# Value products of local attention one tile later and amid the step, scores at its end; the feed-forward mean, variance and broadcast in the other bank

## What is computed

```
def attn_layer(x, Wqkv, qs, ksc, Wo):
    q, k, v = split(x @ Wqkv)                 # 16 heads of 64
    q = l2norm(q) * qs;  k = l2norm(k) * ksc
    q, k = rotary(q), rotary(k)
    out = local_attention(q, k, v)            # windows of 32: 32 queries see 64 keys
    return out @ Wo
def ffn_layer(x, g, bln, W1, b1, W2, b2):
    xn = (x - mean(x)) / sqrt(var(x) + 1e-05) * g + bln
    a, gate = split(xn @ W1 + b1)             # 2 x 341
    return a * gelu(gate) @ W2 + b2
for i in range(6):
    x = attn_layer(shift_tokens(x), ...) + x
    x = ffn_layer(shift_tokens(x), ...) + x
```

## Time and profile before

| | |
|---|---|
| median of three runs | 3652.7 us (3648.79 to 3658.39) |
| profiled execution | 3656.53 us, its span 3654.8 us |
| PE busy | 3287.4 us, 90% of the span |
| DVE / POOL / ACT busy | 2817.2 / 2340.6 / 2230.3 us (77 / 64 / 61%) |
| granted TensorE clock | 0.961 of full speed on average |
| stretches | first stack about 40 to 1700 us, global attention to about 1970 us, second stack about 1975 to 3645 us |

### The profile page before, as it was taken

The page is one execution under the profiler, slowest core; times in us unless marked ns, Lnnn a source line. Parts: engine busy times, 40 slices in busy tenths (PEclk is TensorE's granted clock), DMA queues, the critical chain, the costliest instruction groups (busy, mean ns, idle before and its releaser), DMA issues. The chain is left out here.

```text
span 3654.8 us, 147212 instructions
## 1 busy us (share of the span) xinstructions
PE 3287.4 (90%) x61692; PEld 2149.2 (59%) x61692; DVE 2817.2 (77%) x4178; ACT 2230.3 (61%) x3970; POOL 2340.6 (64%) x2167
## 2 busy tenths in 40 slices
PE   5899999999999999996897899989999999999996
PEld 2566666666666666663223566666666666666664
DVE  4788888887887888882344788877877788888883
ACT  3566676765665666662774566665666566666663
POOL 4677787776776777772003677666666667777761
PEclk8999999999999999997998899999999999999997
DMA  3234334334334333320001233323323333333321
GB/s 118 74 92 112 87 92 117 86 85 115 80 87 112 82 91 97 84 72 18 21 1 31 69 77 93 81 72 92 79 74 92 76 77 94 86 78 96 82 73 32
DMA packets 216859, 289.96 MB, mean 79 GB/s; under 512 B 61068, under 2 KB 105864, under 8 KB 215304
## 3 DMA queue, kind: packets, MB, share of 16 engines
q1 hardware_dynamic: 216200, 280.54, 29.8%
HBM read 43.43 MB, written 10.49 MB: 15 GB/s over the span
## 5 line engine op out<-in xcount | busy, mean ns | idle before, releaser
L1166 POOL TENSOR_TENSOR rot<-t 128x512 f32<-128x512 f32 x768 | 975.1, 1273 | 309.4 <-DVE t L1025 289.7
L1172 POOL TENSOR_TENSOR qkn<-rot,rn 128x512 f32<-128x512 f32 x768 | 793.1, 1043 | 174.7 <-DVE rn L1048 174.7
L1024 DVE TENSOR_TENSOR t<-duo,table 128x512 f32<-128x512 f32 x768 | 526.5, 686 | 156.0 <-ACT sq L854 144.4
L1178 POOL TENSOR_TENSOR prob<-prob,rsum 128x512 f32<-128x512 f32 x192 | 297.0, 1547 | 417.7 <-DVE rsum L1067 417.0
L1025 DVE TENSOR_TENSOR t<-duo,table 128x512 f32<-128x512 f32 x768 | 522.4, 680 | 0.0
L693 PE MATMUL sv_all<-pT,arena 64*64 64x32 f32 x24576 | 419.7, 221 | 82.8 <-issue 82.7
L625 PE MATMUL duo<-w_pair,in_hi 128*128 128x512 f16 x1152 | 452.1, 392 | 34.6 <-POOL in_lo L1193 15.7
L860 ACT ACTIVATE arena<-duo 128x512 f32<-128x512 f32 x384 | 226.8, 591 | 403.5 <-PE duo L627 400.5
L854 ACT ACTIVATE sq<-duo 128x512 f32<-128x512 f32 x768 | 443.7, 600 | 39.9 <-PE duo L627 38.5
L649 PE MATMUL duo<-ident,qkn 128*128 128x128 f32 x3072 | 456.6, 280 | 9.0 <-issue 6.9
L1031 DVE TENSOR_REDUCE n<-sq 128x16 f32<-128x1024 f32 x384 | 464.3, 1209 | 0.0
(11 more groups left out here) (125 smaller groups left out, 5002.8 us busy)
## 6 DMA issues: line engine op xcount, KB each, us to landing
arena<-arena SPq DMA_DIRECT2D x1152, 128.0 KB, 2.4
arena<-arena SPq DMA_DIRECT2D x768, 64.0 KB, 2.0
w_pair<-w_split SPq DMA_DIRECT2D x44, 256.0 KB, 4.2
w_stage<-in_L_ffn_Wqkv SPq DMA_DIRECT2D x6, 1536.0 KB, 8.6
w_split<-split SPq DMA_DIRECT2D x30, 256.0 KB, 2.6
wo_sb<-in_L_ffn_Wo SPq DMA_DIRECT2D x12, 512.0 KB, 4.2
xsh<-xs SPq DMA_DIRECT2D x48, 128.0 KB, 2.5
f_in<-xs SPq DMA_DIRECT2D x48, 128.0 KB, 2.2
```

The source lines that it names most:

```text
L1024: dve.tensor_tensor(t1[:, b, :].rearrange("p (h d) -> p h d", d=DH), src, cos, ALU.mult)
L1166: pool.tensor_tensor(rot[:, c, :], t1[:, c % 2, :], t2[:, c % 2, :], ALU.add).then_inc(pool_add, 1)
L1172: pool.tensor_tensor(qkn[:, 0, c, :].rearrange("p (h d) -> p h d", d=DH), rot[:, c, :].rearrange("p (h d) -> p h d", d=DH), rn[:, c, :].un ...
```

## The change

It moves work between steps and inside a step; the arithmetic is the same.

- `turn_prob` and `outputs` take tile T - 3 instead of T - 2. `turn_prob` comes right after projection 0, `outputs` after `turn_qk` 1 and ahead of projection 2. `scores` stays near the end, so the `sv` banks now go scores, maximum and subtraction, outputs, in turn over two steps. On ACT `store_prob` comes ahead of `exps`, `store_out` ahead of `squares` 2.
- `f_mean`, `f_var` and `f_rep` write the bank `fb` (was `fa`). `f_wo` moves behind projection 3, `f_w2` ahead of projection 1, `f_rep` from behind `turn_qk` 3 to ahead of projection 3.
- On DVE `rotary` 1 comes ahead of `sums`, `rotary` 3 ahead of the second `norm2`, `f_resid1` behind `floor_norm`.
- On POOL `prob_norm` moves from the end of a step to behind `add` 1 of the next one, and `f_rstd` and `f_diag` from the fourth step to the first step of the next batch, behind `prob_norm`.

```
-                def turn_qk(T, c, prob_between=False):
+                def turn_qk(T, c):
+                    pe.wait_ge(*((act_p, tile_done(T - 2, c, 2)) if c < 2 else (act_k, tile_done(T, c - 2, 4))))
...
-                def f_rep(B, wo_between):
-
+                def f_rep(B):
+                    pe.wait_ge(pool_diag, batch_done(B))
+                    pe.matmul(fb[:, :], ones_w[:, :], diag[:, :, :].rearrange("p t c -> p (t c)"),
+                              start=True, stop=True).then_inc(pe_rep, 1)
...
                         project(T, q, s, 0)
-                    if s == 0 and f1:
-                        f_wo(B - 1, L_prev, 0, 0)
+                    if three:
+                        turn_prob(T - 3, (s - 3) % 2, span.tile(s, 2))
                     if s == 1 and f2:
-                        f_gate(B - 2, 0)
+                        f_gate(B - 2, 0, f1)
                         f_up(B - 2, 0)
-                    if s == 2 and f1:
-                        f_wo(B - 1, L_prev, 1, 0)
-                    if s == 3 and f1:
-                        f_mean(B - 1)
+                    if s == 3 and f2:
+                        f_w2(B - 2, f1)
...
+                    if s == 3 and f1:
+                        f_mean(B - 1)
+                    if three:
+                        outputs(T - 3, B if s == 3 else B - 1, (s - 3) % TILES, span.tile(s, 2))
...
-                    if two:
-                        turn_prob(T - 2, s % 2, one)
+                    if s == 0 and f2:
+                        f_rep(B - 2)
...
+                    if s in (0, 2) and f1:
+                        f_wo(B - 1, L_prev, s // 2, 0)
```

ScalarE, VectorE and GpSimd:

```
                     if now:
                         squares(T, 0)
-                    if s == 3 and f1:
-                        f_centre(B - 1)
+                    if three:
+                        store_prob(T - 3)
                     if two:
                         exps(T - 2, s % 2)
...
                     if now:
                         rotary(T, s, 0)
+                        rotary(T, s, 1)
                     if two:
                         sums(T - 2, s % 2)
                         prob_norm(T - 2, s % 2)
...
                     if now:
                         add(T, 1)
+                    if two:
+                        prob_norm(T - 2, s % 2)
+                    if s == 0 and f2:
+                        f_rstd(B - 2)
+                        f_diag(B - 2)
                     if now:
                         add(T, 2)
...
-                    if one:
-                        prob_norm(T - 1, (s - 1) % 2)
```

More of the change, by code:

```diff
@@ L759, in step @@
                     T = B * TILES + s
-                    now, one, two = span.tile(s, 0), span.tile(s, 1), span.tile(s, 2)
+                    now, one, three = span.tile(s, 0), span.tile(s, 1), span.tile(s, 3)
                     f1, f2 = span.batch(1), span.batch(2)
@@ L803, in step @@
                         project(T, q, s, 3)
+                    if s in (0, 2) and f1:
+                        f_wo(B - 1, L_prev, s // 2, 0)
+                    if s == 2 and f2:
+                        f_up(B - 2, 2)
                     if one:
-                        turn_qk(T - 1, 2, two)
-                    if two:
-                        outputs(T - 2, B if s >= 2 else B - 1, (s - 2) % TILES)
+                        turn_qk(T - 1, 2)
+                    if s in (0, 2) and f1:
+                        f_wo(B - 1, L_prev, s // 2, 1)
                     if s == 1 and f2:
@@ L810, in step @@
                     if one:
-                        turn_qk(T - 1, 3, two)
-                    if s == 0 and f2:
-                        f_rep(B - 2, f1)
-                    if s == 2 and f2:
-                        f_up(B - 2, 2)
+                        turn_qk(T - 1, 3)
                     if s == 3 and f1:
@@ L935, in step @@
                     T = B * TILES + s
-                    now, one, two = span.tile(s, 0), span.tile(s, 1), span.tile(s, 2)
+                    now, one = span.tile(s, 0), span.tile(s, 1)
+                    two, three = span.tile(s, 2), span.tile(s, 3)
                     f1, f2 = span.batch(1), span.batch(2)
@@ L957, in step @@
                     if s == 3 and f1:
+                        f_centre(B - 1)
                         f_square(B - 1)
-                    if two:
-                        store_prob(T - 2)
+                    if three:
+                        store_out(T - 3, B if s == 3 else B - 1, (s - 3) % TILES)
                     if now:
@@ L1112, in step @@
                     if now:
-                        rotary(T, s, 1)
                         norm2(T, 0)
-                    if s == 0 and f1:
-                        f_resid1(B - 1, b1x, 0)
+                    if s == 1 and f2:
+                        f_gated(B - 2, 0)
                     if s == 3 and f2:
@@ L1217, in step @@
                     T = B * TILES + s
-                    now, one = span.tile(s, 0), span.tile(s, 1)
-                    f1 = span.batch(1)
+                    now, one, two = span.tile(s, 0), span.tile(s, 1), span.tile(s, 2)
+                    f2 = span.batch(2)
                     if now:
```

83 lines of the change are left out of this document (32 added, 51 removed).

## The result

The changed kernel takes 4023.5 us (median of four runs, 4010.5 to 4026.6) against 3652.0 us before: ratio **1.1004, interval 1.0977 to 1.1031**, about 370 us slower. The profiled execution took 4010.5 us.

A forecast was written before the change was run, and what follows sets the result against it. PE's own order was taken to bound the steps, every other engine just ahead of it. Terms +216, +97, +59, +37, +4 and -66 sum to +347 on 3652.7, giving 4000 us; range 3850 to 4120 for 8 in 10.

The forecast's parts named there:

- The wait for `diag`: First step of a batch: PE stands 4.9 us at `f_rep` until POOL has made `diag`, 44 times, +216 us.
- The clock: After that wait in first steps PE's granted clock falls, costing 2.2 us in each of 44 batches, +97 us.
- The second step: Late `squares` 1 delays `rotary` 2, the first values and `store_v`: 17.0 us against 15.67, 44 times, +59 us.
- The fourth: Fourth step, same chain from `squares` 1 to `store_v`: 15.85 us against 15.02, 44 times, +37 us.
- The third: Third step: `f_wo` behind projection 3 covers the chain, so only +0.1 us a step, +4 us.
- What it gives back: Value product stalls ahead of the new waits vanish, with some clock drops, -66 us; the scores' stalls stay.
- the first (the wait alone, 3807): Rival: the wait stands, but the clock stays and second and fourth steps keep their length; 3807 us, chance 0.20.
- stalls stay beside the waits: Rival: the stalls stay in addition to the new waits, so nothing is given back; 4066 us, chance 0.05.
- worse: Rival: a lower clock in second steps too, and `exps` of first steps delayed; 4141 us, chance 0.12.
- the fall of the clock in second steps: Part of the rival at 4141 us: PE's 1.9 us idle in second steps also lowers the clock, another 97 us.
- the delay of `exps` behind DVE: Part of the rival at 4141 us: DVE's backlog from the fourth step pushes the first's `exps` by 1 us, 44 us.
- Two of the signs: Expected in the profile after: first steps of 21 to 23 us; value products' "issue" idle about as before in sum.

The follow-up runs named there:

- 1: The changed kernel with `f_rstd` and `f_diag` made in the fourth step again, behind the last `normalise` on GpSimd: 3791.3 us, 1.0341.
- 2: The changed kernel with `f_rep` back behind the last `turn_qk` on PE and `f_scale` behind `rotary` 3 on DVE: 3781.2 us, 1.0318.
- 5: The kernel before with only `f_rstd` and `f_diag` in the first step behind `add` 1 and `f_rep` ahead of projection 3: 3971.8 us, 1.0854.
- 6: The kernel before with only `f_rstd` and `f_diag` moved to the first step, `f_rep` left in its old place: 3695.8 us, 1.0100.
- 7: The changed kernel with `f_rstd` and `f_diag` ahead of `prob_norm` in the first step: 3961.1 us, 1.0826.
- kernel 3: The changed kernel with 18 matmuls of 512 columns, results thrown away, on PE between projection 2 and `f_rep`: 3930.9 us, 1.0725.
- kernels 4: The changed kernel with the next layer's weight loads for projections 0 and 1 ahead of the third tile's window copy: 3983.7 us, 1.0860.
- kernel 8: The changed kernel with `f_rstd` and `f_diag` in the fourth step again and the next layer's weight loads ahead of window copies: 3676.9 us, 1.0044.

## Why the prediction was right, and where it wasn't

**The wait for `diag`** (predicted 4.9 us in 44 batches, +216): right in mechanism and place, and near in size. In the step shown PE came at 5.95 (5.7) and `diag` at 11.1 (10.6), but that step is one of the longer waits: the 44 batches have 189 us, 4.3 each, and the drains, which were given nothing, 12 us more, 201.4 in all. Kernels 1 and 2 show that it is this wait, 5 that the pair of moves makes it without the others, 6 and 1 that either half alone makes little of it, and 7 which of the two chains is the one: GpSimd's queue.

**The clock** (+97): right; kernel 3 gives 102 us, 2.3 per batch against 2.2. The wait and the clock together are 201 + 102 = 303 against 313; the pair of kernels 4 and 8 says 299.

**The second step** (+59): the step "it waits 1.9 ... that is 17.0 us" was too large. `squares` 1 ended 5.8 us after the step's start in place of 6.2, the wait for `rotary` 2 was 1.45, and `store_v` cost nothing that I can find behind it: 16.5 us, so 0.83 over the earlier trace rows, 44 x 0.83 = 37. **The fourth** (+37) was 15.96 without stalls instead of 15.85; but the 15.02 that this was set against was too long, as unstalled fourth steps of the kernel before take 14.85, so the growth was 1.11 us and not 0.85. **The third** was given 4 us; its mean grew by 0.70 us, 31 us in all. Most of it is not stalls: the shortest third step grew from 14.92 to 15.41, which is 22 of the 31 us. The largest single piece, by the starts of the rows of such a step, is 0.33 us ahead of the mask matmuls of `scores`, where PE went straight on before. In first and third steps the waits of PE count a part of it as idle time:

```profile
PE sv_all L656 <- issue: 17.2, 95, 0.8
```

No experiment here tells what makes PE pause there.

**What it gives back** (-66): the value products' stalls fell by 30.5 us, not by 51, and the scores' by 4. In second steps it is more than I took: their mean stood 1.50 us over the unstalled length (17.18 against 15.68) and stands 0.31 over it now (16.82 against 16.51). The rule that I had weighed against this term (Runtime: NRT & Kernel Launch of the Trainium skill, section Instruction fetch mechanics: the next block is fetched while one executes and the pace of issue hides it) agrees with most of the places where one block of 256 records gives way to the next, but not with all: 120 of 481 in the two stacks stall for over 0.7 us, 100 of these within scores or value products (the last section), and there the measurement decides against it. All the terms but wait and clock sum to +34 in the prediction; kernel 8 measures them as +16, give or take some 9, with their own clock in it.

**The step that was missing**: SP's queue. The prediction followed the four engines and never asked what else waits for `pe_pv`, which `outputs` raises: the window copies, with the weights of the next layer queued behind. That is +53 us by kernel 4, and 109 once the wait for `diag` no longer covers it.

The sum then is 303 + 53 + 16 = 372 against 370 measured, and 347 predicted: the missing term of +53 against 10 and 18 too much in the others. The agreement to 2 us says less than it seems: kernel 4's 53, the 299 between kernels 4 and 8, and kernel 8's 16 add up to the whole by the way they are measured, so only 303 against 299 is a test, and each difference is uncertain by some 10 to 15 us. That the forecast came within 25 us of the result owes something to luck, as the term that it missed and those that it had too large have opposite signs.

Of the **rivals**, the first (the wait alone, 3807) falls by kernel 3, and "stalls stay beside the waits" is about half true. Of "worse", the fall of the clock in second steps didn't come (3.4 us of it in all of them); the delay of `exps` behind DVE is 0.16 us in the first step shown, and I didn't follow it further. Two of the signs missed: first steps are 23.9 us and not 21 to 23, as the stalls in the scores come on top of wait and clock, and the value products' "issue" time didn't stay "about as before" but fell by 30.5 us. That sign and the term of -66 were at odds in the prediction itself.

**What stays open**: why each value product stall or score stall costs what it does and most borders have none, and what makes PE pause ahead of the mask matmuls.

## What to carry to other kernels

A product that crosses engines has two ends. Moving the maker later cost 1% here, both together 8.5%; the user earlier was not run by itself, but is in kernel 8, which with all the other moves is at 0.4%; so before moving either, write the time at which it is ready beside the time at which it is wanted, from the rows of one step. Then list everything that waits for the moved step's semaphore, DMA queues included, and everything queued behind those waits. And an order on one engine need not be the same in all steps: the one that won here differed between first and second.

## What the runs showed of the hardware

**Dense blocks can outrun the instruction fetch.** The trace has 61,692 matmuls of PE, as many weight loads and 2,329 other records of its own, 125,713 in all; 491 packets of 16 KB of the instruction queue times 256 records are 125,696. Numbered in the order of their starts, 119 of the 122 "issue" stalls over 0.7 us of the kernel before stand ahead of record 193 or 194 of their 256, in the changed kernel 88 of 91, and with 128 records added at the start (kernel 11) 123 of 126: there the stalls kept their place in the count and changed their kind of step. Nine in ten of them are 0.9 to 2.4 us long in the kernel before, and end 2.2 to 2.9 us after the start of a fetch, 1.2 to 1.6 us after its end. A block of 128 value products is 256 records in 2.0 us, the scores' in 1.5 us, so it can use up a packet before the next has come. That it must isn't so: of the 384 such places within scores and value products of the kernel before, 100 stall and 284 don't, and what decides isn't shown here.

**A wait of 4.3 us costs PE half as much again.** In each of the 44 first steps PE stands for 4.3 us on average, the clock is at the lower level for 6.5 us, and each batch lost 2.3 us more by it. Keeping PE at idle work through the wait gave that back, though the time at which `diag` was ready stayed.
